# A four-layer window-attention kernel with its input, weights and output handed over in the layout of the chip's tiles

## The chip, the core and the metric

The kernel runs on one core of a Trainium2 chip. The metric is device time in microseconds (us), lower is better. The kernel before took 8497.35 us as the median of three runs (8497.1 to 8511.64).

Names used below: PE is TensorE (matmuls; PEld its weight loads), DVE is VectorE, ACT is ScalarE, POOL is GpSimd, SP is SyncE, which computes nothing and issues DMAs. ACT and POOL issue DMAs too. A row "SPq" or "ACTq" with DMA_DIRECT2D is the issue of transfers, not the transfer itself.

## What is computed

The input x is 16 images of 56 x 56 tokens with 96 channels, float32. Four transformer layers of shifted-window attention follow each other, each of this shape (layers differ in norm, number of heads and mask):

```
def layer(x, mask, qkv, table, proj, mlp):
    h = norm(x)                                      # layer 0: over the whole image; others: per token
    h = roll(h, (-3, -3)); xw = windows(h, 7, 7)     # 64 windows of 49 tokens per image
    q, k, v = split(xw @ qkv_w + qkv_b)              # 12, 12, 12 and 4 heads
    a = softmax(q @ k.T * scale + rel_bias(table) + mask)
    h = roll(unwindow((a @ v) @ proj_w + proj_b), (3, 3))
    x = x + h
    return x + (gelu(norm(x) @ w1 + b1) @ w2 + b2)   # layer 3 has one more norm before w2
```

The mask of layer 0 is an input (one 49 x 49 table for each window of each image); those of layers 1 to 3 are constants. The roll by (-3, -3) and the cut into windows are the same in all four layers.

## The kernel before

The 16 images are worked in four groups of four. The tile `x` holds two groups; in it a partition is one of 98 tokens (two windows side by side, 2 x 49) and the free dimension runs over the group's 128 window pairs and 96 channels. So the rolled and windowed form is made once, when x is loaded, and undone once, when the output is stored: everything between works in place. Four window pairs make a quad; an attention stage or an MLP stage of a layer is 32 quads. Each engine has its own program: `fill` for the first two quads, then a loop over the four groups with, for each layer, 32 quads of attention and 32 quads of MLP, software-pipelined (`quad_steps`, `rolled_steps`, `mlp_into_attention`). Within the loop PE, DVE, ACT and POOL hand tiles to each other by semaphores, and SP issues, for every attention quad, four copies `Vbd<-Vd` (L524) and in layer 0 two mask loads (`mask_quad`, L436).

Where x and the output move: `tokens` (L429) cuts four images by `runs` into 312 DMAs, each of 7, 4 or 3 partitions (a row of a window, or its two parts where the roll wraps) and up to 32 window pairs of 96 channels, 384 bytes a piece. The first group is loaded at the start, half of its DMAs by SP and half by ACT, images 0 and 1 first (`s_x0`), then images 2 and 3 (`s_x`). In the loop SP stores group g-1 after the spreads of layer 0's attention, and loads group g+1 after those of layer 1; both lie beside MLP stages, in which SP has no spreads to issue. At the very end SP stores images 0 and 1 of the last group while their last layer still runs for images 2 and 3, then waits for `s_fin` (the last group is finished) and stores images 2 and 3 together with ACT.

What precedes the loop: POOL sets the pads (memsets L560 to L568: the zeros around blocks of `mask0`, `Vbd` and the staged tables, and the ones that stand in as a bias row in `hT`, `OT`, `h4`), then issues the tables of relative bias (`load_bias`, L488: 49 DMAs a layer, 7 partitions each, straight from the 13 x 13 tables into their 49 x 49 form) and the weights of layer 2. SP and ACT issue the other weights (`load_weights`, L443, 18 DMAs a layer) and ACT the first table, behind their parts of x. Four copies `room<-room` (L579) double the staged tables to the second window's partitions (64 to 112). DVE takes the first mean and variance of each token as x lands (L1042, L1050, L1056; 32 quads), waits for all constants, folds the gain of layer 3's extra norm into `w3` (L1078 to L1088, with two short matmul groups L840 and L842 on PE between), and writes the bias tables (L1101: layer 0; L1103: layers 1 to 3, staged table plus constant mask, once for each of four mask cases and each of two windows, 49 partitions each; the source is read backwards along the keys). Then come the image norm of layer 0 (`norm`: L1137 to L1178 on DVE, averages L862 on PE behind warming matmuls L856, a power on POOL L588), the first ACT instruction (L745), and the loop.

Of the kernel before, what the change touches and what calls it, by code (L numbers as in the profile page):

```python
# [13 lines left out]
N = WS * WS  # L14
# [93 lines left out]

def build(nc, d, x_in, out):
    ctx = ExitStack()  # L110
    with ctx:
# [72 lines left out]
        s_braw0 = sem("first_bias_raw_loaded")  # L184
        s_bsec = sem("bias_raw_copied")
        s_tab = sem("bias_tables_ready")
        s_memset = sem("pads_set")
        s_x = sem("x_loaded")
        s_x0 = sem("first_images_loaded")
        s_const2 = sem("third_layer_loaded")  # L190
# [204 lines left out]
        def runs(first, last):  # L395

            A = NWR
            for r in range(WS):  # L400
                if r + SHIFT < WS:
                    rows = [(slice(first * A, last * A), first * H + r + SHIFT)]
                else:
                    rows = [(slice(m * A, m * A + A - 1), m * H + r + SHIFT) for m in range(first, last)]
                    rows.append((slice(first * A + A - 1, last * A, A), first * H + r + SHIFT - WS))
                for a, row in rows:
                    for w in range(2):
                        for j in range(4):
                            cut = WS if w == 0 else WS - SHIFT
                            q = N * w + WS * r  # L410
                            col = WS * (2 * j + w) + SHIFT
                            yield slice(q, q + cut), a, j, row, col
                            if w:
                                yield slice(q + cut, q + WS), a, j, row, (col + cut) % W

        def tokens(eng, g, store, s, first=0, last=IMGS, turn=0, turns=1):

            dram = out if store else x_in
            rows_of = x[:, bass.ds((g % 2) * NP, NP), :].rearrange("p (a j) c -> p a j c", j=4)
            for n, (q, a, j, row, col) in enumerate(runs(first, last)):  # L420
                if n % turns != turn:
                    continue
                step = a.step or 1
                count = len(range(a.start, a.stop, step))
                far = bass.AP(dram.tensor, g * (IMGS * H * W * C) + (row * W + col) * C,
# [11 lines left out]

        TOK_DMAS = len(list(runs(0, IMGS)))
        HALF_DMAS = len(list(runs(0, IMGS // 2)))
        n_const, n_const2 = [0], [0]  # L440

        def load(eng, dst, src):
            eng.dma_start(dst, src).then_inc(s_const, 16)  # L443
# [961 lines left out]
```

## Time and profile before

| | |
|---|---|
| median of three runs | 8497.35 us |
| profiled execution: its own time, and its span | 8497.1 us, 8497.1 us |
| PE busy | 7930.6 us, 93% of the span |
| DVE, POOL, ACT busy | 72%, 64%, 61% |
| DMA moved | 142.33 MB in 597322 packets, 596066 of them under 512 B |
| issues of x and the output | 312 DMAs for a group, each way |

The profiled execution has a span equal to its own time, so its rows can be laid against the time of the runs directly. The share of DMA in a row of windows is the mean busy share of the core's 16 DMA engines. Read the table with the stages in mind: the first 165.8 us and the last 44.6 us of the span have hardly any PE work in them, while the middle is a periodic loop.

### The profile page before, as it was taken

The numbers are of one execution on the slowest core, as the hardware profiler recorded it, in microseconds if no ns is written. First come the engines' busy times: TensorE is split into PE (matmuls) and PEld (weight loads), VectorE is DVE, ScalarE is ACT, GpSimd is POOL, SyncE is SP. The second block draws the span as 40 slices with busy tenths as digits, with TensorE's granted clock in tenths as the row PEclk, the third lists the DMA queues.
The fourth block names the chain that finished last, engine by engine and source line by source line (L and its number), as shares of the span: only waits on it lengthen the run. The fifth ranks groups of instructions, "written<-read, shape, count | busy, mean of one in ns | idle before, by whom it ended". The sixth has DMA issues, their size and how long they took to land.

```text
span 8497.1 us, 316211 instructions
## 1 busy us (share of the span) xinstructions
PE 7930.6 (93%) x111222; PEld 5968.4 (70%) x111222; DVE 6104.5 (72%) x18304; ACT 5155.3 (61%) x9130; POOL 5402.6 (64%) x6733
## 2 busy tenths in 40 slices
PE   2999999999999999999999999999999999999997
PEld 1777777777777777776767777777776777777766
DVE  3777767767777776776777677776677767777666
ACT  1755747646774664755767476574577647566456
POOL 6865646556785665655778465564678756566565
PEclk9999999999999999999999999999999999999998
DMA  3100010000011011000001101000101100000001
GB/s 42 22 13 10 15 27 15 10 12 13 10 21 31 13 20 23 15 7 16 9 15 21 28 15 28 15 15 4 20 3 21 26 21 15 6 14 13 7 17 23
DMA packets 597322, 142.33 MB, mean 17 GB/s; under 512 B 596066, under 2 KB 596662, under 8 KB 596877
## 3 DMA queue, kind: packets, MB, share of 16 engines
q1 hardware_dynamic: 574508, 131.49, 7.8%
q10 hardware_dynamic: 16865, 3.97, 0.3%
q8 instruction: 246, 4.03, 0.2%
q0 software_dynamic: 5504, 1.21, 0.1%
q14 instruction: 199, 1.63, 0.1%
HBM read 31.76 MB, written 19.27 MB: 6 GB/s over the span
## 4 chain that ended last, share of the span: by engine, by line
PE 70%; DVE 12%; issue 8%; ACT 3%; DVEq 3%; POOL 1%; POOLq 0%; ACTq 0%
PE ps L912 12%; PE ps L973 11%; PE ps L900 8%; PE ps L876 7%; PE ps L1016 7%; PE ps L989 7%; PE ps L919 5%; PE ps L942 3%; PE ps L952 3%; DVE bst L1042 3%; ACT PT L779 3%; PE ps L961 2%; DVE xn L1195 2%; PE ps L856 2%; DVE S L1244 2%
## 5 line engine op out<-in xcount | busy, mean ns | idle before, releaser
L643 POOL TENSOR_TENSOR S<-S,mx 113x588 f32<-113x588 f32 (+1 forms) x2048 | 2065.4, 1008 | 1528.3 <-DVE mx L1246 1524.5
L779 ACT ACTIVATE PT<-ps 98x588 f32<-98x588 f32 (+1 forms) x2048 | 1182.5, 577 | 1239.9 <-PE ps L973 1233.1
L912 PEld LDWEIGHTS ps<-Vbd,PT 98*49 98x49 f32 x40960 | 1113.0, 125 | 666.4 <-issue 642.7
L1244 DVE TENSOR_TENSOR S<-ps,bias 113x588 f32<-113x588 f32 (+1 forms) x1536 | 962.9, 627 | 856.7 <-PE ps L900 856.7
L912 PE MATMUL ps<-Vbd,PT 98*49 98x18 f32 (+1 forms) x40960 | 1326.7, 202 | 171.7 <-ACT PT L779 109.7
L1246 DVE TENSOR_REDUCE mx<-S 113x12 f32<-113x588 f32 (+1 forms) x2048 | 1359.6, 664 | 70.5
L973 PEld LDWEIGHTS ps<-ident,S 113*98 113x98 f32 x10240 | 1040.6, 128 | 473.1 <-issue 382.0
L973 PE MATMUL ps<-ident,S 113*98 113x113 f32 x10240 | 1346.0, 262 | 3.8 <-ACT S L761 3.4
L761 ACT ACTIVATE S<-S 113x588 f32<-113x588 f32 (+1 forms) x2048 | 1240.0, 605 | 54.4 <-POOL S L643 52.3
L989 PEld LDWEIGHTS ps<-w,G 128*98 128x98 f32 x12288 | 1151.1, 168 | 161.6 <-issue 89.5
L989 PE MATMUL ps<-w,G 128*98 128x96 f32 (+1 forms) x12288 | 1152.0, 250 | 0.8 <-DVE x L1329 0.8
L1016 PE MATMUL ps<-h,w 97*128 97x392 f32 x3072 | 1125.6, 503 | 9.1 <-ACT G L819 9.1
L900 PE MATMUL ps<-room,QT 32*64 32x196 f32 (+3 forms) x26624 | 1054.1, 311 | 11.1 <-issue 10.8
L1042 DVE BATCH_NORM_STATS2 bst<-x 98x6 f32 (+1 forms) x4224 | 869.7, 253 | 178.9 <-DMA x<-x_dram 80.4
L732 ACT ACTIVATE room<-ps,kmask 96x392 f32<-96x392 f32 x1540 | 887.5, 578 | 44.8 <-PE ps L876 44.8
L819 ACT ACTIVATE G<-ps 128x1176 f32<-128x1176 f32 x512 | 588.8, 1150 | 536.0 <-PE ps L1016 535.7
L876 PE MATMUL ps<-hT,wqkv 97*96 97x392 f32 (+1 forms) x2052 | 891.3, 517 | 18.7 <-ACT hT L784 10.1
L609 POOL TENSOR_TENSOR rstd<-rstd,neghalf 98x4 f32 (+1 forms) x768 | 787.6, 1025 | 143.9 <-POOL rstd L606 143.9
L1016 PEld LDWEIGHTS ps<-h,w 97*128 97x128 f32 x3072 | 549.4, 192 | 302.4 <-ACT G L819 12.3
L797 ACT ACTIVATE h<-ps,gb 96x392 f32<-96x392 f32 x512 | 345.5, 675 | 638.0 <-PE ps L1003 638.0
L627 POOL TENSOR_TENSOR G<-bias,mask 113x588 f32<-113x588 f32 x513 | 688.0, 1341 | 7.8 <-issue 7.6
L900 PEld LDWEIGHTS ps<-room,QT 32*64 32x64 f32 (+1 forms) x26624 | 443.6, 123 | 342.3 <-issue 340.6
(104 smaller groups left out, 10493.0 us busy)
## 6 DMA issues: line engine op xcount, KB each, us to landing
Vbd<-Vd SPq DMA_DIRECT2D x1536, 41.3 KB
Vbd<-Vd SPq DMA_DIRECT2D x512, 38.3 KB
mask<-L_conv_mask_matrix_dram SPq DMA_DIRECT2D x258, 37.5 KB
x<-x_dram SPq DMA_DIRECT2D x48, 84.0 KB
out_dram<-x SPq DMA_DIRECT2D x48, 84.0 KB
x<-x_dram SPq DMA_DIRECT2D x228, 10.5 KB
out_dram<-x SPq DMA_DIRECT2D x228, 10.5 KB
out_dram<-x SPq DMA_DIRECT2D x180, 18.4 KB
```

Source lines behind the costliest of these rows:

```text
L643: pool.tensor_tensor(v, v, m, ALU.subtract).then_inc(a_sub, 1)
L761: act.activation(S[:, e, 0:nh * N], S[:, e, 0:nh * N], ACT.Exp).then_inc(a_exp, 1)
L779: act.activation(PT[:, (s + 3) % 4, 0:blocks, :, :].rearrange("p (b t) w n -> p b (t w) n", b=banks), PTps[:, PT_BANK[l] - 3:PT_BANK[l] - ...
L876: return pe.matmul(dst[0:at.stop - at.start, :], wqkv[:, at], hT[:, :, :, :].rearrange("p j w n -> p (j w n)"), start=True, stop=True)
L900: last = pe.matmul(out, q, keys, start=True, stop=True)
L912: last = pe.matmul(Ops[ROW2 * w:ROW2 * w + N, p, b, :].rearrange("p (a n) -> p a n", a=2), PT[:, p, b, w, :], v, start=True, stop=True)
L973: last = pe.transpose(at.rearrange("p w q -> p (w q)")[:, 0:TOK], S[:, e, PAIR * b:PAIR * (b + 1)], ident[0:TOK, 0:TOK])
L989: last = pe.matmul(ps[0:PAIR, 6 + t, wide * j:wide * j + weights.shape[1]], G[:, t, c, PAIR * j:PAIR * (j + 1)], weights, start=(c == 0), ...
L1016: last = pe.matmul(ps[:, 2 + c, 0:QUAD * PAIR], w1[:, l, P * c:P * (c + 1)], h4[:, s, :, :].rearrange("p a q -> p (a q)"), start=True, sto ...
L1042: last = dve.bn_stats(bst[:, t, j, :], x[:, half + (at + j), :])
L1244: dve.tensor_tensor(dst, scores, b, ALU.add).then_inc(a_bi, 1)
L1246: dve.reduce_max(mx[:, e, 0:nh], S[:, e, 0:n].rearrange("p (h k) -> p h k", k=N), axis=AX.X).then_inc(a_mx, 1)
```

## The change

The host hands over x already rolled, cut into windows and laid out as [group, 98 partitions, 128 pairs x 96], and takes the output back in that layout (`to_windows`, `from_windows`). So `tokens` is one DMA for each image: 98 partitions of 32 x 96 floats (12,288 contiguous bytes), four for a group instead of 312. The weights of all layers are handed over side by side, with each bias vector as row 97 of its matrix: `wqkv` is one DMA of 97 partitions x 1216 floats, `w1` one of 97 x 1536, `wp` one of 97 x 384; `w2`, `c2`, `gb`, `gb3` are one DMA each. Layer 0's bias table comes finished (`bias0`, 128 x 588), the others as one staged tile (128 x 1372), with both windows' rows in it and the keys in order, so the copies `room<-room` and layer 0's table copy are gone and DVE adds the constant masks over all 128 partitions at once. The mask of layer 0 is laid out so that a partition's four windows are contiguous. POOL keeps three small memsets; the pads of `mask0`, `hT`, `OT`, `h4` and `Vbd` are set by DVE at the head of its program. Neither the host's packing nor its unpacking is in the device time.

```
     def tokens(eng, g, store, s, first=0, last=IMGS, turn=0, turns=1):
         dram = out if store else x_in
-        rows_of = x[:, bass.ds((g % 2) * NP, NP), :].rearrange("p (a j) c -> p a j c", j=4)
-        for n, (q, a, j, row, col) in enumerate(runs(first, last)):
-            if n % turns != turn:
...
-            far = bass.AP(dram.tensor, g * (IMGS * H * W * C) + (row * W + col) * C,
-                          [[C, q.stop - q.start], [step * WS * W * C, count], [1, C]])
-            near = rows_of[q, a, j, :]
+        for image in range(first, last):
+            if image % turns != turn:
+                continue
+            at = slice(image * PAIRS_IMG, (image + 1) * PAIRS_IMG)
+            far = dram[g, :, at.start * C:at.stop * C]
+            near = x[:, (g % 2) * NP + at.start:(g % 2) * NP + at.stop, :].rearrange("p a c -> p (a c)")
             dst, src = (far, near) if store else (near, far)
             eng.dma_start(dst, src).then_inc(s, 16)
...
     def _(sp):
         tokens(sp, 0, False, s_x0, 0, IMGS // 2, turn=0, turns=2)
         tokens(sp, 0, False, s_x, IMGS // 2, IMGS, turn=0, turns=2)
-        load(sp, ident[:, :], d["ident"])
-        load(sp, kmask[:, :], d["kmask"])
         load(sp, average[:, :], d["average"])
-        sp.wait_ge(s_memset, 1)
-        for l in (0, 3):
-            load_weights(sp, l, load)
...
+        load(sp, w1[:, :, :].rearrange("p l n -> p (l n)"), d["w1"])
+        load(sp, c2[:, :, :].rearrange("p l n -> p (l n)"), d["c2"].to_broadcast([P, LAYERS * C]))
+        load(sp, gb3[:, :, :].rearrange("p j c -> p (j c)"), d["gb3"])
+        sp.wait_ge(s_maskpad, 1)
...
     def _(pool):
-        for t in (mask0, room, Vbd):
-            pool.memset(t[:], 0.0)
...
-        for l in range(1, LAYERS):
-            load_bias(pool, l, s_braw)
...
-        for l in range(LAYERS):
-            pool.dma_start(stage(l)[ROW2:ROW2 + N, :], stage(l)[0:N, :]).then_inc(s_bsec, 16)
+        pool.wait_ge(s_memset, 2)
...
     def _(act):
-        act.wait_ge(s_memset, 1)
-        load_bias(act, 0, s_braw0)
-        load_weights(act, 1, load)
+        load(act, ident[:, :], d["ident"])
+        load(act, kmask[:, :], d["kmask"])
+        load(act, wqkv[:, :], d["wqkv"])
+        load(act, gb[:, :, :].rearrange("p l j -> p (l j)"), d["gb"])
+        load(act, wp[:, :, :].rearrange("p l n -> p (l n)"), d["wp"])
+        load(act, w2[:, :, :, :].rearrange("p l c n -> p (l c n)"), d["w2"])
+        load(act, bias[0][:, 0, :], d["bias0"])
+        load(act, mask4[:, :, :].rearrange("p a b -> p (a b)"), d["mask4"])
+        act.dma_start(room[:, 0:STAGED], d["bias"]).then_inc(s_braw, 16)
...
     def _(dve):
+        dve.memset(mask0[:], 0.0).then_inc(s_maskpad, 1)
+        for t in (hT, OT, h4):
+            dve.memset(t[:], 1.0)
+        dve.memset(Vbd[:], 0.0).then_inc(s_memset, 1)
         dve.wait_ge(s_x0, 16 * HALF_DMAS)
...
-        for l in range(LAYERS):
+        for l in range(1, LAYERS):
             nh = HEADS[l]
-            for v in range(1 if l == 0 else 4):
-                for w in range(2):
-                    r = slice(ROW2 * w, ROW2 * w + N)
-                    dst = bias[l][r, v, :].rearrange("p (h k) -> p h k", k=N)
-                    src = stage(l)[r, :].rearrange("p (h k) -> p h k", k=N)[:, :, ::-1]
...
+            for v in range(4):
+                last = dve.tensor_tensor(bias[l][:, v, :].rearrange("p (h k) -> p h k", k=N),
+                                         stage(l).rearrange("p (h k) -> p h k", k=N),
+                                         mask4[:, v, :].unsqueeze(1).to_broadcast([P, nh, N]), ALU.add)
```

How the order of instructions moves is shown at three places. In the rows, "7x2x96 x2" is the shape of one DMA (partitions first) and how many follow each other.

The end of ACT's issues before the loop, in the kernel before (the last of its 156 DMAs for x, the table of layer 0, the weights of layer 1, and its first computing instruction):

```order
L429 DMA x<-x_dram 7x2x96 x2
L429 DMA x<-x_dram 3x2x96 x4
L488 DMA room<-L_conv_rel_bias_table_dram 7x12x7 x49
L443 DMA wqkv<-L_conv_qkv_w_dram 96x96 x2
L443 DMA wqkv<-L_conv_qkv_w_dram 96x6x8 x2
L443 DMA wqkv<-L_conv_qkv_b_dram 1x96 x2
L443 DMA wqkv<-L_conv_qkv_b_dram 1x6x8 x2
L443 DMA wp<-L_conv_proj_w_dram 96x96
L443 DMA wp<-L_conv_proj_b_dram 1x96
L443 DMA w<-L_conv_mlp_w_dram 96x384
```

The whole of ACT's issues before the loop in the changed kernel:

```order
L460 DMA x<-x_dram 98x3072 x2
L473 DMA ident<-k_ident_dram 128x128
L473 DMA kmask<-k_kmask_dram 96x4
L473 DMA wqkv<-wqkv_dram 97x1216
L473 DMA gb<-gb_dram 96x16
L473 DMA wp<-wp_dram 97x384
L473 DMA w<-w_dram 128x1152
L473 DMA bias<-bias_dram 128x588
L473 DMA G<-k_mask_dram 128x196
L693 DMA room<-bias_dram 128x1372
L721 ACT_TABLE_LOAD
L721 ACTIVATE xn<-x,nmr,vpe 98x384
```

ACT issues 11 DMAs in place of 223 there; the weights of all layers stand in tiles of 96, 97 or 128 partitions.

DVE between the token statistics and the loop, before (`gb`, `w`: layer 3's extra norm; `bias<-room,G`: the tables, `G` holding the constant mask):

```order
L1078 MEMSET room 128x128
L1079 MEMSET w 128x3
L1081 COPY room<-gb 128x128 x3
L1083 TENSOR_SCALAR w<-w,gb 128x96 x3
L1086 TENSOR_TENSOR w<-w,ps 128x3x96
L1088 TENSOR_TENSOR c<-c,ps 128x96
L1101 COPY bias<-room 49x588 x2
L1103 TENSOR_TENSOR bias<-room,G 49x588 x16
L1103 TENSOR_TENSOR bias<-room,G 49x196 x8
L1204 MEMSET Vd 98x48
```

The same place in the changed kernel, from the last two steps of the norm's part:

```order
L1063 TENSOR_TENSOR w<-w,ps 128x3x96
L1065 TENSOR_TENSOR c<-c,ps 128x96
L1071 TENSOR_TENSOR bias<-room,G 128x588 x8
L1071 TENSOR_TENSOR bias<-room,G 128x196 x4
L1173 MEMSET Vd 98x48
```

Twelve additions over 128 partitions stand for twenty-four additions and two copies over 49.

The end of SP's program before, after the last spread (the last rows of its stores of images 2 and 3):

```order
L429 DMA out_dram<-x 7x7x96 x2
L429 DMA out_dram<-x 4x7x96 x4
L429 DMA out_dram<-x 7x2x96 x2
L429 DMA out_dram<-x 4x2x96 x4
L111 UNCONDITIONAL_BRANCH
```

The end of SP's program in the changed kernel:

```order
L511 DMA Vbd<-Vd 49x4x50 x4
L306 REGISTER_ALU
L306 COMPARE_AND_BRANCH
L511 DMA Vbd<-Vd 49x4x50 x4
L460 DMA out_dram<-x 98x3072 x3
L168 UNCONDITIONAL_BRANCH
```

Three DMAs (images 0, 1 and 2; image 3 is ACT's one) stand where SP had 234. Inside the loop PE, DVE, ACT and POOL have the same instructions in the same order as before; on SP only `tokens` and the shape of the mask loads differ.

## Rows read from the trace of the kernel before

**Rows 1.** The page: span, busy time, PE and DMA in 40 slices.

```profile
span 8497.1 us, 316211 instructions
PE 7930.6 (93%) x111222; PEld 5968.4 (70%) x111222; DVE 6104.5 (72%) x18304; ACT 5155.3 (61%) x9130; POOL 5402.6 (64%) x6733
PE   2999999999999999999999999999999999999997
DMA  3100010000011011000001101000101100000001
```

**Rows 2.** Waits, whole run: engine line waited for: us in total, times, longest.

```profile
ACT L745 <- DVE nmr L1178: 165.8, 1, 165.8
DVE bst L1042 <- DMA x<-x_dram: 80.4, 2, 56.1
```

**Rows 3.** Timeline, start of the program: start us, us, what, [idle before <- releaser].

```profile
0.76 90.71 SPq L429 DMA_DIRECT2D x<-x_dram  x156
...
56.09 1.38 DVE L1042 BATCH_NORM_STATS2 bst<-x 98x6 f32<-98x96 f32 x8 [56.09 <-DMA x<-x_dram]
...
79.44 0.17 DVE L1056 COPY mv<-agg 98x8 f32<-98x8 f32 x1
...
103.93 1.38 DVE L1042 BATCH_NORM_STATS2 bst<-x 98x6 f32<-98x96 f32 x8 [24.32 <-DMA x<-x_dram]
...
127.24 0.17 DVE L1056 COPY mv<-agg 98x8 f32<-98x8 f32 x1
...
135.02 0.17 DVE L1078 MEMSET room<- 128x128 f32 x1 [7.62 <-DMA gb<-L_conv_norm_b_dram]
...
139.71 0.93 DVE L1101 COPY bias<-room 49x588 f32<-49x588 f32 x2
...
156.23 0.10 DVE L1204 MEMSET Vd<- 98x48 f32 x1
```

**Rows 4.** Groups by form, 0 to 170 us: x count | busy us, mean ns.

```profile
L1103 DVE TENSOR_TENSOR bias<-room,G 49x588 f32<-49x588 f32 x16 | 12.3, 766 | 0.2
L1103 DVE TENSOR_TENSOR bias<-room,G 49x196 f32<-49x196 f32 x8 | 2.9, 357 | 0.1
L1164 DVE TENSOR_SCALAR ivar<-ps 98x4 f32<-98x4 f32 x1 | 0.2, 161 | 3.4 <-PE ps L862 3.4
```

**Rows 5.** The line of DVE's largest memset: duration ns min/median/max.

```profile
L1208 DVE MEMSET ps<- x16: 485/485/485, 174.6 to 7990.1; 128x512 f32 x16
```

**Rows 6.** Windows: PE, PEld, DVE, ACT, POOL busy, PE clock, DMA share, GB/s.

```profile
12.00:22.00 10.00, 0.00 (x0) 0.00 (x0) 0.00 (x0) 0.00 (x0) 9.69 (x21) 1.00 0.44 62
104.00:105.00 1.00, 0.00 (x0) 0.00 (x0) 1.00 (x7) 0.00 (x0) 1.00 (x3) 1.00 0.86 146
131.00:132.00 1.00, 0.00 (x0) 0.00 (x0) 0.00 (x0) 0.00 (x0) 0.00 (x0) 1.00 0.86 289
140.00:160.00 20.00, 8.59 (x14) 3.67 (x15) 17.44 (x33) 0.00 (x0) 0.00 (x0) 0.76 0.00 0
8455.00:8495.00 40.00, 0.00 (x0) 0.00 (x0) 0.00 (x0) 0.00 (x0) 0.00 (x0) 0.50 0.26 58
```

**Rows 7.** DMA issues, 0 to 170 us: count, KB each, median us to landing.

```profile
room<-conv_rel_bias_table_dram POOLq DMA_DIRECT2D x98, 2.3 KB, 3.2
room<-room POOLq DMA_DIRECT2D x3, 112.5 KB, 2.7
```

**Rows 8.** Timeline, end of the program.

```profile
8449.37 1.36 DVE L1329 SCALAR_TENSOR_TENSOR x<-ps,r,x 98x96 f32 x4
...
8452.51 42.68 SPq L429 DMA_DIRECT2D out_dram<-x  x78
```

**Rows 9.** Windows: the MLP stage of layer 0 in groups 0 and 3, of layer 1 in groups 0 and 3.

```profile
567.00:719.00 152.00, 141.06 (x1050) 111.04 (x1049) 103.70 (x437) 58.84 (x65) 68.90 (x96) 1.00 0.00 0
...
6779.00:6931.00 152.00, 141.37 (x1051) 111.34 (x1052) 104.78 (x439) 58.65 (x65) 70.36 (x96) 1.00 0.13 27
1103.00:1250.00 147.00, 141.23 (x1047) 111.04 (x1048) 101.73 (x430) 58.60 (x65) 72.18 (x99) 1.00 0.16 27
7315.00:7462.00 147.00, 141.25 (x1048) 111.08 (x1049) 101.57 (x430) 58.63 (x65) 72.58 (x99) 1.00 0.00 0
```

**Rows 10.** SP's timeline around the load of group 1.

```profile
1001.73 83.64 SPq L524 DMA_DIRECT2D Vbd<-Vd  x32
1085.41 112.21 SPq L429 DMA_DIRECT2D x<-x_dram  x228
```

More of the change, by code:

```diff
@@ new lines, in packed @@
+def packed(inputs):
+    out = {"x": to_windows(inputs["x"])}
+    m = inputs["L0_conv_mask_matrix"].reshape(B * PAIRS_IMG, 2, N, N).transpose(1, 2, 0, 3)
+    out["mask"] = m.reshape(2, N, B * PAIRS_IMG * N)
+    qkv, p, m1, m2, last, gains, bias = [], [], [], [], [], [], []
+    for l in range(LAYERS):
+        w = {r: inputs[n] for r, n in names(l).items()}
+        if l == 2:
+            w = {r: a.T if r in ("wqkv", "wp", "w1", "w2") else a for r, a in w.items()}
+        full = np.concatenate([w["wqkv"], w["bqkv"][None]])
+        dh = C // HEADS[l]
+        for j in range(2):
+            part = full[:, C * j:C * (j + 1)]
+            if HEADS[l] == 4:
+                part = np.pad(part.reshape(C + 1, 4, dh), ((0, 0), (0, 0), (0, GRP - dh))).reshape(C + 1, P)
+            qkv.append(part)
+        v = full[:, 2 * C:].reshape(C + 1, HEADS[l] // 2, 2, dh)
+        qkv.append(v.transpose(0, 2, 1, 3).reshape(C + 1, C))
+        p.append(np.concatenate([w["wp"], w["bp"][None]]))
+        m1.append(np.concatenate([w["w1"], w["c1"][None]]))
+        m2.append(w["w2"].reshape(HC, P, C).transpose(1, 0, 2).reshape(P, HC * C))
+        last.append(w["c2"])
+        gains += [w["g1"], w["b1"], w["g2"], w["b2"]]
+        t = w["table"][index_of_bias()].transpose(0, 2, 1).reshape(N, HEADS[l] * N)
+        rows = np.zeros((P, HEADS[l] * N), np.float32)
+        rows[0:N], rows[ROW2:ROW2 + N] = t, t
+        bias.append(rows)
+    out["wqkv"] = np.concatenate(qkv, axis=1)
+    out["wp"], out["w1"], out["w2"] = (np.concatenate(a, axis=1) for a in (p, m1, m2))
+    out["c2"] = np.concatenate(last)[None]
+    out["gb"] = np.stack(gains, axis=1)
+    out["gb3"] = np.concatenate([inputs[n].reshape(HC, P).T for n in ("L3_conv_ln3_g", "L3_conv_ln3_b")], axis=1)
+    out["bias0"] = bias[0]
+    out["bias"] = np.concatenate(bias[1:], axis=1)
+    return out
@@ L444, in load @@
             n_const[0] += 16
[L446 to L488 removed]
+        STAGED = sum(HEADS[1:]) * N
+        def stage(l):
+            return room[:, sum(HEADS[1:l]) * N:sum(HEADS[1:l + 1]) * N]
         @block.sync
@@ L1400 @@
         d[name] = d.pop("k_" + name)
[L1401 removed]
+    out = nc.dram_tensor("out_0_dram", (GROUPS, PAIR, NP * C), F32, kind="ExternalOutput").ap()
     build(nc, d, d["x"], out)
     r = _run(nc, [arrays], core_ids=[0])
[L1404 removed]
+    return from_windows(np.asarray(r.results[0]["out_0_dram"]))
```

126 lines of the change are left out of this document (23 added, 103 removed).

## The prediction, made before the changed kernel ran

> **What bounds the kernel now.** I read the page first [rows 1]. PE is busy 93% of the span and no other engine passes 72%, so in the middle of the program only PE's work counts. But the 40 slices of PE read 2, then 9 throughout, then 7: the first slice of 212 us is mostly empty, and so is part of the last. The change touches only DMAs and what surrounds them, so those two ends are where to look.
>
> The list of waits names the front end [rows 2]: ACT's first instruction waits 165.8 us, and DVE waits 80.4 us in two pieces for x. The timeline of the start shows how these come about [rows 3]. SP issues its 156 DMAs for x in 90.71 us (0.58 us each), as ACT does beside it. DVE can begin the token statistics of images 0 and 1 at 56.09, ends them at 79.61, and waits for images 2 and 3 until 103.93; those statistics end at 127.41. The last constant (layer 1's `gb`, issued by ACT behind its x and the table of layer 0) lets DVE go on at 135.02. Then come 4.69 us of folding the extra norm of layer 3 (to 139.71), 16.5 us of bias tables (to 156.23), and 9.55 us of image norm, to 165.78.
>
> The timeline of the end [rows 8]: DVE's last residual of layer 3 ends at 8450.73, SP and ACT begin to issue images 2 and 3 at 8452.51, and the span ends at 8497.1, so 44.6 us of pure output stand behind the last arithmetic. The profiled execution's own time is its span, 8497.1, and the median is 8497.35, so the sum below needs no correction.
>
> **The middle of the program: nothing.** In the loop SP issues x and the output after its last spread of a stage: the load of group 1 follows 32 spread DMAs directly, takes 112.21 us [rows 10], and lies beside an MLP stage of 147 us, so SP is free again before the next spread is due. Did the transfers themselves slow the stage? Layer 1's MLP in group 0 runs with such a load beside it (DMA share 0.16) and in group 3 with none (0.00): 1047 matmuls and 141.23 us of PE against 1048 and 141.25 [rows 9]. Layer 0's MLP without a store in group 0 and with one in group 3: 141.06 against 141.37. So the 312 issues cost the loop nothing now, and removing them gives nothing. The mask loads keep their number. Instructions on the other engines are unchanged. What can get worse is the intensity, a rival below.
>
> **The transfer of x at the start.** An image is 98 partitions x 12,288 bytes = 1.204 MB; four are 4.82 MB. How many DMA engines carry a DMA from SP or ACT? While both issue only pieces of 7, 4 and 3 partitions the share is 0.44, that is 7 of 16 engines (0.4375), and while tiles of 96 and 128 partitions are in flight it is 0.86 [rows 6]. I read this as: a DMA is dealt to its engines in equal whole numbers of partitions. 98 partitions then go to 14 engines, 7 each: 86 KB an image on each engine, 172 KB for two images, 344 KB for four.
>
> At what rate? At the end of the program, with 384-byte pieces, 58 GB/s at a share of 0.26 is 13.9 GB/s for a busy engine (27.6 ns a piece). With the 2,352-byte rows of `room<-room` it is 289 GB/s at 0.86, or 21.0 GB/s (112 ns) [rows 6]. A fixed part and a part by size through these two points give 0.043 ns a byte, so my estimate for rows of 4.9 to 12 KB is 23 GB/s an engine. As fixed time of a DMA I take 3.2 us from issue to landing, from the small table DMAs [rows 7]. So images 0 and 1 are in at 0.8 + 172/23 + 3.2 = 11.5 us instead of 56.09. The two statistics stretches (23.52 and 23.48 us, [rows 3]) then follow each other without a gap and end at 58.5.
>
> **DVE's pads** stand ahead of this: 392 + 392 + 392 + 784 + 1728 elements a partition at 485 ns for 512 [rows 5] are 3.5 us, over before x lands at 11.5. If that cover were gone they would cost 3.5. POOL's memsets never held anybody and give nothing back.
>
> **The weights are the next late thing.** `wqkv`, `w1` and `wp` now have 97 partitions, and 97 has no divisor that is 16 or less but 1. Dealt as above, all of 97 x 4,864 + 97 x 6,144 + 97 x 1,536 = 1.217 MB goes through one engine, which also carries its 344 KB of x and about 81 KB of the 128-partition constants due before `s_const`: 1,642 KB. SP's `w1` and ACT's `wqkv` and `wp` are on two queues but, so read, on the same engine, so they add. At 23 GB/s: 0.8 + 71.4 + 3.2 = 75.4 us, behind the statistics at 58.5. The start is thus bound by one DMA engine. The staged tables (44 KB more on it, 1.9 us) land within the 4.69 us of folding. Bounds: if the 97 partitions spread over the engines, the constants are in well before 58.5; if the engine keeps the 13.9 GB/s of small pieces, they are in at 122.1.
>
> The Trainium skill, "DMA: Bandwidth & Descriptors" (section "Why a DMA increments its semaphore by 16 and not by 1"), states such a rule: the number of engines is the largest up to 16 that divides the slowest dimension of both sides, with 127 partitions as an example for one engine. The share of 0.44 agrees for 7 partitions; no row shows 97. By the rule the sum is the one I take, without it that of the second case below. The same page puts an engine at about 27 GiB/s (29 GB/s); an estimate by that would be constants at 60.6 us and 8378 us in all.
>
> **From the constants to the loop.** Folding stays 4.69 us. Tables: before, 16 additions at 766 ns, 8 at 357 and two copies [rows 4]. Now 8 and 4 over 128 partitions; free size and operation are the same, so 8 x 0.766 + 4 x 0.357 = 7.6 us instead of 16.5. At the price of the copies (0.93 us for two, [rows 3]), were the backward read what made them slow, they would be some 3 us cheaper; if the cost rose with partitions (128/49), 12 us dearer. I take equal, since free size sets all of DVE's durations that I see. The norm stays 9.55. In it DVE waits 3.4 us for PE's warming matmuls and average [rows 4], in a stretch where the granted clock is 0.76 on average [rows 6], a mixture of full and half (2.4 and 1.2 GHz), after PE had stood idle for the tables. With shorter tables PE idles less; 0 to 2 us may come back, I count 0.
>
> So the loop starts at 75.4 + 4.7 + 7.6 + 9.5 = 97.2 instead of 165.8: 68.6 us less.
>
> **The end.** Images 0 and 1 are stored under the last MLP stage, as before. For images 2 and 3, 172 KB an engine: 7.5 + 3.2 = 10.7 us after 8452.51 instead of 44.6: 33.9 less. At 13.9 GB/s it is 15.6, so 29.0 less. Sum: 8497.1 - 68.6 - 33.9 = 8394.6 us.
>
> **Rivals.**
> 1. *One engine carries the 97-partition weights* (the forecast): 8395. For it: the shares. Against: it rests on pieces of 7 partitions.
> 2. *The weights spread; DVE's statistics bind.* Constants are in before 58.5, and the loop starts at 58.5 + 21.8 = 80.3: 85.5 + 33.9 less, 8378. For it: 0.86 with large tiles, partly from POOL's queue, whose dealing may differ.
> 3. *Long rows bring no better rate.* 13.9 GB/s: constants at 122.1, loop at 143.9, 21.9 + 29.0 less, 8446. Against: the 21.0 GB/s of the copies; for it: those are between tiles of the chip, not from memory.
> 4. *Slower: the single engine takes its rows one after another, with their latency.* ACT's queue holds 194 such rows (`wqkv`, `wp`). At the 2.7 us from issue to landing of the large copies [rows 7] a row, constants come at about 528 us and the time is about 8847. It decides from 0.9 us a row in ACT's queue, where the start is 34 us later than now and eats the gain at the end. Against: 62 GB/s over 7 engines in 384-byte pieces is one in 43 ns an engine [rows 6], far below any latency.
> 5. *The bursts in the loop stop PE.* A group now moves in about 4.82 MB / (14 x 23 GB/s) = 15 us, at twice the share seen beside PE or more. Six and a half such bursts with PE standing throughout cost 97 us: 8492, no change. Against: rows 9, which see no loss at all at the lower intensity.
>
> **How the numbers follow.** The forecast has 68 in 100, the second case 17, the third 8, the fourth 2, the fifth 2; 3 are left for mixtures. Predicted is the forecast's 8394. Its own unknown is the engine's rate: at 17 GB/s it gives constants at 100.6, a tail of 13.3 and 8422. Downward the second case with 4 us less for tables and norm gives 8374. The range 8373 to 8422 leaves out cases 3 to 5. 0.2% is 17 us, about what a measurement of this kernel can tell from no change: faster by more holds for cases 1 to 3 and the mixtures, 96 in 100; within it case 5, 2; slower case 4, 2.
>
> **What would show it.** Right: ACT's first instruction near 97 us; DVE's first statistics near 11 with a single wait for x, a gap of some 17 us between the last statistics (58) and L1055, put down to a DMA; 7.6 us of L1071; in the windows from 25 to 75 us a DMA share near 1/16 with 20 to 25 GB/s; a last store issued about 11 us before the end; a group's period unchanged. If the share stays high until the constants are in, near 30 us, and L1055 follows the statistics at once, the second case holds. If the window after 25 us shows 14 GB/s or less, the third. The prediction is wrong in kind if the MLP stages of layers 0 and 1 grow, or if the loop starts after 165.8.

## The result, and the profile after

| | before | after |
|---|---|---|
| median (lowest to highest) of 4 runs each | 8501.19 us (8497.1 to 8511.64) | 8372.33 us (8370.18 to 8374.06) |
| span of the profiled execution | 8497.1 us | 8371.6 us |
| start: ACT's first instruction | 165.8 us | 91.8 us |
| from there to the issue of the last stores | 8286.7 us | 8269.8 us |
| from there to the end | 44.6 us | 10.0 us |

After over before is 0.9847, with a 95% interval of 0.9833 to 0.9861: the changed kernel is faster by 1.5%. The spans differ by 125.5 us, and the table divides them: 74.0 at the start, 16.9 in the loop, 34.6 at the end. The prediction had 68.6, nothing and 33.9, in all 8394 with a range of 8373 to 8422. (The medians of the four runs differ by 128.9.) So the time is 22 us better than predicted and just under the range. Most of the miss is the 16.9 us of the loop, where the prediction saw nothing to gain: without them the time would be 8389, 5 us better than predicted and inside the range.

The page of the changed kernel (answers to [rows 1]):

```profile
span 8371.6 us, 313958 instructions
PE 7933.7 (95%) x111222; PEld 5970.4 (71%) x111222; DVE 6097.4 (73%) x18295; ACT 5156.9 (62%) x9130; POOL 5299.7 (63%) x6553
PE   6999999999999999999999999999999999999998
```

PE has the same 111,222 matmuls and 3 us more busy time than before, in a span 125 us shorter; the first slice of PE went from 2 to 6. All of the gain is idle time of PE.

Its waits, whole run (answers to [rows 2]; engine, line, what it waited for, us in total, times, longest):

```profile
ACT L721 <- DVE nmr L1147: 91.8, 1, 91.8
DVE room L1055 <- DMA G<-k_mask_dram: 13.2, 1, 13.2
DVE bst L1017 <- DMA x<-x_dram: 7.9, 1, 7.9
```

The two waits for x (80.4 us) became one of 7.9, and a wait for the constants, 13.2 us, is there in its place.

Its timeline of the start (answers to [rows 3]; start us, us, what, idle before and its releaser). x12 in the row at 77.43 counts both forms:

```profile
0.76 0.84 SPq L460 DMA_DIRECT2D x<-x_dram  x2
...
2.37 26.94 SPq L473 DMA_DIRECT2D c<-c_dram  x1
3.25 29.74 ACTq L473 DMA_DIRECT2D gb<-gb_dram  x1
3.26 1.50 DVE L1049 MEMSET Vbd<- 98x1728 f32 x1 [0.31 <-issue]
12.61 1.38 DVE L1017 BATCH_NORM_STATS2 bst<-x 98x6 f32<-98x96 f32 x8 [7.86 <-DMA x<-x_dram]
...
36.05 1.38 DVE L1017 BATCH_NORM_STATS2 bst<-x 98x6 f32<-98x96 f32 x8
36.44 25.40 ACTq L473 DMA_DIRECT2D w<-w_dram  x1
...
59.32 0.17 DVE L1031 COPY mv<-agg 98x8 f32<-98x8 f32 x1
...
62.52 0.48 ACTq L473 DMA_DIRECT2D G<-k_mask_dram  x1
63.03 0.48 ACTq L693 DMA_DIRECT2D room<-bias_dram  x1
72.75 0.17 DVE L1055 MEMSET room<- 128x128 f32 x1 [13.25 <-DMA G<-k_mask_dram]
...
77.43 6.63 DVE L1071 TENSOR_TENSOR bias<-room,G 128x588 f32<-128x588 f32 x12
...
88.68 0.16 DVE L1133 TENSOR_SCALAR ivar<-ps 98x4 f32<-98x4 f32 x1 [1.37 <-PE ps L837]
```

The second half of the statistics follows the first at 36.05 without a gap. They end at 59.5, and DVE then stands until 72.75. Three issues last 25 to 30 us each, and one of ACT (`wp`) and five of SP behind the first of them 3.4 us each, where the others last 0.2 to 0.6. The trace names nothing that an issue waits for; that it waits for room in a queue is a reading. So the last constants, `G` and the staged tables, were issued only at 62.52 and 63.03, and landed some 10 and 11 us later.

Windows of the changed kernel (columns as in [rows 6]), of the start, the norm and the end:

```profile
5.00:10.00 5.00, 0.00 (x0) 0.00 (x0) 0.00 (x0) 0.00 (x0) 0.00 (x0) 1.00 0.86 297
15.00:20.00 5.00, 0.00 (x0) 0.00 (x0) 3.96 (x32) 0.00 (x0) 0.00 (x0) 1.00 0.77 243
50.00:55.00 5.00, 0.00 (x0) 0.00 (x0) 3.71 (x28) 0.00 (x0) 0.00 (x0) 1.00 0.06 26
...
80.00:92.00 12.00, 11.61 (x27) 4.94 (x26) 7.42 (x20) 0.24 (x1) 2.90 (x3) 1.00 0.00 1
8365.00:8371.00 6.00, 0.00 (x0) 0.00 (x0) 0.00 (x0) 0.00 (x0) 0.00 (x0) 0.50 0.68 262
```

Two plateaus: up to 20 us most engines work, and at 50 us the share is 0.06, one engine of 16, moving 26 GB/s. By the Trainium skill's "DMA: Bandwidth & Descriptors" (section "Why a DMA increments its semaphore by 16 and not by 1") 97 partitions go to a single engine, since 97 has no divisor up to 16 but 1; the 0.06 agrees. At the end (0.68, 262 GB/s) the stores of images 2 and 3 take 10.0 us in place of 44.6 [rows 8].

The loop is where the unexpected part lies. Windows from the first to the last matmul of `h` times `w1` in the MLP stages of layers 0, 2 and 1, first group; the kernel before (for layers 0 and 1 this is [rows 9] cut exactly):

```profile
567.09:719.17 152.08, 141.15 (x1050) 110.98 (x1049) 103.61 (x437) 58.75 (x65) 68.98 (x96) 1.00 0.00 0
1635.84:1785.22 149.38, 140.51 (x1046) 110.56 (x1044) 101.28 (x430) 58.52 (x64) 71.85 (x99) 1.00 0.00 0
1103.27:1250.07 146.80, 141.03 (x1046) 110.77 (x1044) 101.46 (x429) 58.55 (x64) 72.22 (x99) 1.00 0.15 27
```

and the changed kernel:

```profile
489.31:637.45 148.14, 141.15 (x1050) 110.99 (x1049) 103.95 (x438) 58.52 (x64) 70.58 (x96) 1.00 0.00 0
1553.00:1700.85 147.85, 140.71 (x1045) 110.61 (x1044) 101.42 (x430) 58.53 (x64) 72.34 (x99) 1.00 0.00 0
1022.08:1168.42 146.34, 140.53 (x1046) 110.58 (x1045) 101.22 (x429) 58.52 (x64) 72.09 (x99) 1.00 0.00 0
```

The same matmuls, the same PE busy time, no DMA beside them in layers 0 and 2, full clock; yet layer 0's stage is 3.9 us shorter and layer 2's 1.5, while layer 1's hardly differs. Over the four groups the stages of layer 0 add up to 14.0 us and those of layer 2 to 6.0 us less; the rest of the loop gives back 3 to 4. Where in a stage? One turn of the two-quad loop of layer 0, DVE's normalization at the turn, in the kernel before:

```profile
628.25 1.40 DVE L1195 TENSOR_SCALAR xn<-x,mv,vpe 98x96 f32 x4 [0.72 <-issue]
...
629.70 0.54 PE L1003 MATMUL ps<-ident,xn 98*96 98x98 f32 x4 [0.56 <-DVE xn L1195]
```

and after:

```profile
548.71 1.39 DVE L1164 TENSOR_SCALAR xn<-x,mv,vpe 98x96 f32 x4 [0.55 <-issue]
...
550.16 0.54 PE L978 MATMUL ps<-ident,xn 98*96 98x98 f32 x4 [0.30 <-DVE xn L1164]
```

"issue" means that DVE waited for nothing that the profile shows: it is the time in which it branches back to the head of its loop and the next instruction begins. It is 0.17 us shorter, PE's wait for `xn` is 0.26 us shorter, and a turn of PE (two quads) takes 9.34 us instead of 9.58. The loop makes 13 such turns in a stage; each is at least 0.24 us shorter, the first two 0.38 and 0.54, and together they are the 3.9 us. Nothing in the code of the loop accounts for it: DVE's instructions and their order are the same.

The records of DVE's sequencer in the same traces show two places where the time goes. From the end of the branch back to the beginning of the next instruction pass 0.26 us before and 0.11 after. And one of the four statistics of the turn's second quad begins 0.10 us later before than after, so that the four take 1.01 us instead of 0.91:

```profile
625.66 1.01 DVE L1042 BATCH_NORM_STATS2 bst<-x 98x6 f32 x4
```

```profile
546.40 0.91 DVE L1017 BATCH_NORM_STATS2 bst<-x 98x6 f32 x4 [0.16 <-DVE x L1319]
```

The two together are the 0.24 us of a turn.

### The profile page after: what moved, and what is told of

The parts are those of the page before. It is cut to its first block, busy times and chain, and to the rows that moved or that the text cites. A ratio compares the mean times of both kernels' runs of the same rounds, so it can differ in the third digit from the quotient of the medians.

```text
span 8371.6 us, 313958 instructions
## 1 busy us (share of the span) xinstructions
PE 7933.7 (95%) x111222; PEld 5970.4 (71%) x111222; DVE 6097.4 (73%) x18295; ACT 5156.9 (62%) x9130; POOL 5299.7 (63%) x6553
## 4 chain that ended last, share of the span: by engine, by line
PE 68%; DVE 12%; issue 9%; POOL 4%; ACT 3%; DVEq 3%; POOLq 0%; ACTq 0%
PE ps L887 12%; PE ps L948 10%; PE ps L991 7%; PE ps L964 7%; PE ps L875 7%; PE ps L851 7%; PE ps L894 5%; PE ps L917 3%; PE ps L927 3%; DVE bst L1017 3%; ACT PT L755 2%; POOL G L597 2%; PE ps L936 2%; DVE xn L1164 2%; PE ps L831 2%
## 5 line engine op out<-in xcount | busy, mean ns | idle before, releaser
L875 PE MATMUL ps<-room,QT 32*64 32x196 f32 (+3 forms) x26624 | 1054.1, 311 | 11.5 <-issue 11.2
## 6 DMA issues: line engine op xcount, KB each, us to landing
room<-bias_dram ACTq DMA_DIRECT2D x1, 686.0 KB, 11.3
```

Of the source, the lines that this page charges most:

```text
L875: last = pe.matmul(out, q, keys, start=True, stop=True)
```

## Experiments

The theories on the loop, before any experiment: **P**, what changed is where DVE's loops stand in its stream of instructions (DVE executes 567 instructions ahead of its first clearing of PSUM before, 556 after, and the loops are moved by as many); **T**, the lighter DMA traffic or SP's shorter program does it. On the start: **S**, one engine carries the 97-partition weights and everything behind them; against it, that x's transfer or DVE's own work sets the start.

"Loop" below is the time from the start of the first score matmul to the start of the last matmul of `h` times `w1`: 8259.3 us before, 8242.6 after, in the profiled executions. Eight of the runs only add instructions that do nothing (`stand`: an increment of a semaphore that nobody waits for) to DVE's program ahead of everything.

**e1: after, with DVE's loops put back to the place that they had before.**

```diff
     def _(dve):
+        for _ in range(11):
+            stand(dve)
         dve.memset(mask0[:], 0.0).then_inc(s_maskpad, 1)
```

> The changed kernel with 11 idle semaphore increments at the head of DVE's program, where DVE waits for x anyway, so that DVE's loops stand at the same place in its instruction stream as in the kernel before (by the two traces DVE executes 567 instructions ahead of its first L1208 before, 556 after). Theory P (the loop got 17 us shorter because DVE's code moved and its jump back fetches differently): layer 0's MLP stages grow from 148.1 to about 152 us, layer 2's from 147.9 to 149.4, and the time rises by 10 to 20 us to about 8388. Theory T (the loop got shorter because of fewer and larger transfers): stages stay at 148.1 and 147.9, time 8372. Start and end stay as in the changed kernel (91.8 and 10 us).

Measured: median 8385.23 us (8384.5 to 8388.16), 0.9863 of before (0.9846 to 0.9879); loop 8258.1. ACT starts at 90.8, so the eleven instructions cost the start nothing. The stages of layers 0 and 2 are back at the length of before:

```profile
490.01:642.02 152.01, 141.14 (x1050) 110.97 (x1048) 104.52 (x438) 58.54 (x64) 69.85 (x96) 1.00 0.00 0
1558.67:1708.08 149.41, 140.51 (x1046) 110.57 (x1045) 101.34 (x430) 58.54 (x64) 71.81 (x99) 1.00 0.00 0
```

Eleven idle instructions in 8,370 us take back 15.5 of the 16.7 us. Theory T is refuted: the traffic here is that of after, the loop that of before. The 1.2 us left are within what kernels with the same place differ by (see below).

**e2: before, with DVE's loops moved on by 245.** If only the place modulo some power of two counts, 245 = 256 - 11 puts them where they are after.

```diff
     def _(dve):
+        for _ in range(245):
+            stand(dve)
         dve.wait_ge(s_x0, 16 * HALF_DMAS)
```

> The kernel before with 245 idle semaphore increments at the head of DVE's program, ahead of its first wait for x (56 us long, so they should be hidden); 245 is 256 less 11, so if a place in the instruction stream counts modulo 256 instructions or a divisor of it, DVE's loops stand as in the changed kernel. Theory P: layer 0's MLP stages fall from 152 to about 148 us, layer 2's from 149.4 to 147.9, the time to about 8480. Theory T: no change, 8497 to 8505. If neither and the place matters in another way, the stages move by another amount.

Measured: 8479.41 us (8477.23 to 8487.34), 0.9976 of before (0.9966 to 0.9986); loop 8240.9. The two stages, in the kernel with the old DMAs:

```profile
564.62:712.81 148.19, 141.15 (x1049) 110.99 (x1048) 103.99 (x438) 58.45 (x64) 70.48 (x96) 1.00 0.00 0
1628.27:1776.51 148.24, 141.16 (x1045) 110.75 (x1044) 101.51 (x430) 58.49 (x64) 72.23 (x99) 1.00 0.00 0
```

The kernel before gains the whole of the loop's difference without any part of the change (layer 2's stage is 148.2 us in the first group, 147.4 to 147.9 in the other three). P holds in both directions.

**p8 to p256: after, with 8, 16, 32, 64, 128 and 256 idle instructions** (as e1, with another number; each ran once).

> The same with 8 increments (564). If blocks are of 8 or fewer instructions, the stages are those of the changed kernel (148.1, 147.9); if they are of 16 or more, they differ by 1 to 4 us in layer 0 or 2, as 11 increments did. The transfers are the same in all, so any difference is one of place.

> The changed kernel with 16 idle semaphore increments at the head of DVE's program (572 DVE instructions ahead of the first L1208's counterpart in place of 556). If DVE's fetch after the jump back of a loop goes in blocks of 16 instructions or fewer, the loops stand in their blocks as in the changed kernel and layer 0's MLP stage stays at 148.1 us, layer 2's at 147.9, time 8372; if blocks are larger, the stages move, to anything between 148 and 152.

> The changed kernel with 32 idle semaphore increments at the head of DVE's program (588 DVE instructions ahead of the first clear of PSUM in place of 556). 8 and 16 increments both lengthened layer 0's MLP stage to about 151.5 us, 256 less 11 on the kernel before did not. If the place counts modulo 32, layer 0's MLP stays at 148.1 and layer 2's at 147.9; if not, 151 to 152 and 149.4.

> The same with 64 increments (620). Modulo 64 or 32: 148.1 and 147.9. If this one and the one with 32 are both long, the period is 128 or 256 instructions.

> The changed kernel with 128 idle semaphore increments at the head of DVE's program (684 in place of 556). Modulo 128: the MLP stages are the changed kernel's, 148.1 us in layer 0, 146.4 in layer 1, 147.9 in layer 2. Modulo 256: at least one of them differs by over 1 us.

> The same with 256 increments (812). By either reading the stages are the changed kernel's: 148.1, 146.4, 147.9; the time is about 8372 if the increments end before x lands at 12.6 us, and later by what they take beyond that. If the stages differ, the place doesn't count modulo 256 and the match of the kernel before with 245 was chance.

Measured (stages of the first group, from windows as above):

| idle instructions | time | loop | MLP of layer 0, 1, 2 |
|---|---|---|---|
| 0 (after) | 8372.33 | 8242.6 | 148.1, 146.3, 147.9 |
| 8 | 8380.56 | 8249.8 | 152.3, 146.4, 149.4 |
| 11 (e1) | 8385.23 | 8258.1 | 152.0, 146.8, 149.4 |
| 16 | 8385.96 | 8255.0 | 152.0, 146.4, 149.8 |
| 32 | 8387.24 | 8256.3 | 151.5, 146.4, 146.8 |
| 64 | 8384.93 | 8254.1 | 151.7, 148.1, 146.4 |
| 128 | 8375.45 | 8244.4 | 148.2, 146.5, 147.7 |
| 256 | 8373.65 | 8238.8 | 148.1, 146.4, 147.8 |

The lengths of all three stages come back at 128 and at 256 and at no smaller number, and each stage has its own good and bad places. One number is not exact: the stages of layer 0 differ by up to 1.6 us from group to group in the same run (148.1, 149.2, 149.8, 148.1 in after), and over all four groups they add up to 594.4 to 595.2 us with 0, 128 and 256, and to 601.6 to 609.0 with the five others. 64 is the telling one: layer 0 is bad, layer 1 becomes bad, layer 2 is better than ever. The whole-run sum of DVE's idle time ahead of this instruction follows: the rows of before, of after, and of 64. With 128 it is 140.0 us again.

```profile
DVE xn L1195 <- issue: 150.8, 324, 0.7
```

```profile
DVE xn L1164 <- issue: 139.9, 320, 0.7
```

```profile
DVE xn L1166 <- issue: 157.9, 326, 1.2
```

So the place counts modulo 128 instructions of DVE. The sequencer's records say more than the lengths. The loop of an MLP stage is 64 DVE instructions long. In the first group of every run, counting the instructions of a turn from 0, one of them begins late or none does, and the branch back takes more or less time with it (the number after the semicolon: from the end of the branch to the next beginning):

| DVE instructions ahead | runs | layer 0 | layer 1 | layer 2 |
|---|---|---|---|---|
| 556, 684, 812 | after, e3, e5, b2, b3; 128; 256, e2 | none; 0.11 | none; 0.13 | no. 17; 0.22 to 0.24 |
| 544 | b1 | none; 0.13 | none; 0.13 | none seen; 0.24 |
| 564 | 8 | no. 57; 0.26 | none; 0.13 | no. 9; 0.24 |
| 567 | before, e1, e4 | no. 54; 0.26 | none; 0.13 | no. 6; 0.24 |
| 572 | 16 | no. 49; 0.26 | none; 0.13 | no. 1; 0.24 |
| 588 | 32 | no. 33; 0.26 | none; 0.13 | none; 0.13 |
| 620 | 64 | no. 1; 0.26 | no. 41; 0.24 | none; 0.13 |

The late instruction begins about 0.10 us late (0.03 in layer 0 with 8). In each layer its number and the number of instructions ahead add up to the same sum, modulo 128: 621, 661 and 573. By that sum b1's layer 2 should have its pause at no. 29, where none is seen, though its branch back is long. So the pause stands at a fixed place of DVE's stream, one every 128 instructions; a 64-instruction loop either holds such a place or does not, and one that does also branches back 0.10 to 0.15 us later. Layer 2's loop holds one both before and after; there it moved from no. 6, within the four `xn` that PE waits for, to no. 17, a statistic, and the stage is 1.5 us shorter. What in the chip stands behind these places no run shows, nor whether the other engines have them.

Kernels with the same place agree: the eight with loops at 556, 684 or 812 have 8238.7 to 8244.4 us from first to last, the three at 567 have 8258.1 to 8260.6. The 256 also show that idle instructions are not free: they end at 26.2 us, the pads behind them when x has long landed, and the statistics end behind the constants; the start is 4 us later.

**e3: after, the three 97-partition loads cut into 96 and 1.** Its DVE program is unchanged, so its loops stand where those of after stand.

```diff
-        load(sp, w1[:, :, :].rearrange("p l n -> p (l n)"), d["w1"])
+        for rows in (slice(0, C), slice(C, C + 1)):
+            load(sp, w1[rows, :, :].rearrange("p l n -> p (l n)"), d["w1"][rows, :])
```

(and likewise `wqkv` and `wp` on ACT)

> The changed kernel with wqkv, w1 and wp each loaded as two DMAs, 96 partitions and 1 partition, in place of one of 97. Theory E (97 partitions go through one DMA engine and that sets the start): the DMA share no longer sits near 1/16 from 20 to 60 us, the constants are in before DVE's statistics end at 58.5, L1055 follows at about 59.5 without a wait, ACT's first instruction at about 78.5 in place of 91.8, time 8359. Theory B (the start is bound by the bytes or the issue of these loads, not by the engine): L1055 stays near 72 and the time near 8372.

Measured: 8360.21 us (8357.97 to 8362.99), 0.9834 of before (0.9818 to 0.9851), 12 us better than after; ACT starts at 80.6, loop 8238.7. Its windows and its issues:

```profile
5.00:10.00 5.00, 0.00 (x0) 0.00 (x0) 0.00 (x0) 0.00 (x0) 0.00 (x0) 1.00 1.02 263
30.00:35.00 5.00, 0.00 (x0) 0.00 (x0) 3.86 (x32) 0.00 (x0) 0.00 (x0) 1.00 0.80 274
```

```profile
2.90 0.36 SPq L473 DMA_DIRECT2D c<-c_dram  x1
...
3.58 0.32 ACTq L473 DMA_DIRECT2D gb<-gb_dram  x1
...
61.59 0.17 DVE L1058 MEMSET room<- 128x128 f32 x1
```

The share stays high until everything is in (0.80 from 30 to 35 us, 0.03 from 35 to 40). The same issues of `c` and `gb` take 0.36 and 0.32 us in place of 26.94 and 29.74, and L1058 (L1055 of after) follows the statistics with no wait. S holds: the single engine bound the start of the changed kernel. How much of it was its own transfers and how much the issues held up behind them, this run doesn't separate. What it gave is not the 13.2 us of the wait but 11.2: the statistics begin at 14.66 instead of 12.61, with x and the weights now on the same engines.

**e4: before, with only x and the output in the new layout** (`tokens`, `to_windows`, `from_windows` of after; weights, tables, pads as before).

> The kernel before with only x and the output in the layout of windows (four DMAs a group); weights, tables, pads and masks as before. Statistics end at about 60 us; POOL's 147 table DMAs at 0.56 us and its weights then set the constants at about 108, the loop starts at about 139 (27 us earlier than before), the tail falls to 10 us. Theory P: the loop is as long as before, time about 8436. Theory T (the transfers of x shortened the loop): 17 us less, 8419.

Measured: 8440.6 us (8435.11 to 8442.89), 0.9926 (0.991 to 0.9943); start 142.0, loop 8260.6, that of before, as P has it for a DVE program whose loops stand at 567. DVE waits 12.6 us for x, and then:

```profile
DVE room L1066 <- DMA gb<-L_conv_norm_b_dram: 50.6, 1, 50.6
```

x alone brings 23.8 us of the 74.0 at the start; then the constants are late, at 110.17: POOL issues its 147 table DMAs until 98.33 and its weights until 108.35. The end, 10.2 us from the issue of the last stores, is that of after.

**e5: the counterpart, after with x and the output in the old layout.**

> The changed kernel with x and the output as before (312 DMAs a group), weights, tables, masks and pads as changed. The x DMAs fill SP and ACT to about 91 us; only then are the weights issued, with the 97-partition ones on one engine for 1.2 MB / 26 GB/s = 47 us, the rest behind them: constants at about 150 us, the loop starts at about 169 in place of 165.8, the tail is 44.6. Theory P (place in DVE's stream, as in the changed kernel): loop 17 us shorter than before, time about 8484. Theory T (transfers of x shorten the loop): loop as before, about 8500.

Measured: 8464.72 us (8460.95 to 8470.62) where 8484 was expected, 0.9959 (0.9945 to 0.9973); start 149.1 where some 169 was expected, loop 8240.1. The loop is short with the 312 DMAs in it: P again. The two halves of the change don't add up: x alone brings 23.8 us at the start, everything else alone 16.7, both 74.0, since with either alone the other is what comes last. The start was mis-estimated. SP's issues of x:

```profile
0.77 72.54 SPq L484 DMA_DIRECT2D x<-x_dram  x156
```

The same 312 DMAs take 72.5 us here and 90.71 before [rows 3]. Before, POOL's table DMAs, also of 7 partitions, ran beside them; here there are none. That these were on the same seven engines fits the shares (0.37 here between 12 and 22 us, 0.44 before) but was not separated from other differences of the two kernels.

**b1: a better version, first try.** e3, the tables on POOL, the folding moved between the halves of the statistics, and the last store cut: image 2 goes as soon as it is finished, image 3 in halves on SP and ACT.

```diff
+            pool.wait_ge(s_braw, 16)
+            pool.wait_ge(s_const, ALL_CONST)
+            for l in range(1, LAYERS):
+                for v in range(4):
+                    last = pool.tensor_tensor(bias[l][:, v, :]..., stage(l)..., mask4[:, v, :]..., ALU.add)
...
+            sp.wait_ge(m_res, GROUPS * LAYER_QUADS - NQ // 4)
+            tokens(sp, GROUPS - 1, True, s_out, IMGS // 2, IMGS - 1)
             ...
-            tokens(sp, GROUPS - 1, True, s_out, IMGS // 2, IMGS, turn=0, turns=2)
+            last_half(sp, 0)
```

> A version built on the loads in 96 and 1 partitions: POOL, idle at the start, makes the bias tables while DVE takes the statistics (12 additions, hidden; saves DVE 6.7 us); the first half of folding layer 3's norm comes between the two halves of the statistics, so that PE's 3 us of answer are hidden; at the end image 2 is stored by itself when it is done and image 3 in two halves by SP and ACT (tail 10 to about 6.5 us). Against 8360 of the loads in 96 and 1: 8360 - 6.7 - 3 - 3.5 = 8347, if DVE's loops stand well; if their place (12 instructions and some waits fewer) falls badly, up to 17 more, 8364. If POOL and DVE disturb each other in the statistics, DVE's statistics grow above 23.5 us a half.

Measured: 8364.49 us (8363.4 to 8368.21), 0.9841 (0.9825 to 0.9858), where 8347 was expected: no better than e3, though the end alone gives 3.8 us. The end is 6.2 us in place of 10.0. The start is 82.5, later than e3's 80.6, though DVE has 6.6 us less to do:

```profile
35.39 12.39 POOL L568 TENSOR_TENSOR bias<-room,G 128x588 f32<-128x588 f32 x12 [34.47 <-DMA room<-bias_dram]
40.58 2.64 DVE L1081 COPY room<-gb 128x128 f32<-128x128 f32 x2
43.14 3.15 DVE L1083 TENSOR_SCALAR w<-w,gb 128x96 f32<-128x96 f32 x3
```

While POOL adds, DVE's copies take 2.64 us for two (0.35 in after) and its three products 3.15 us (0.62 in after). Later DVE waits 5.4 us for the first average, which PE gives behind its warming matmuls. The loop is 8245.7: this DVE program is 12 instructions shorter (544 ahead), and layer 0's first stage (149.3) is again another; its branch back takes 0.13 us, with no late instruction.

**b2: b1 with the folding back in its place and 12 idle instructions for the 12 additions.**

> b3 with the bias tables made by POOL during DVE's second half of statistics, the fold left where it was (in the combined version it collided with POOL and took 7 us in place of 1), the first group of PE's warming matmuls ahead of the first average left out (there DVE waited 5.4 us for it), and 12 idle increments on DVE for the 12 additions taken away, so that its loops stand at 556. Start 80.6 - 6.6 = 74 to 76, time 8350. If the loop is longer than 8242, place was not restored; if the start is near 80, something else (PE, POOL) took the tables' place.

Measured: 8355.66 us (8348.31 to 8358.36), 0.9823 (0.9807 to 0.984); start 80.3, loop 8242.8. The place is right again, but the statistics end at 65.8 instead of 61.5 in e3: they begin 0.9 us later, and take 3.4 us longer with POOL's additions beside them. In the norm DVE waits 3.4 us for PE where it had waited 1.4. So nearly all of the 6.6 us taken from DVE are given back.

**b3: only e3's cut and the cut last store.**

> The loads in 96 and 1 partitions (8360), and only the end changed: image 2 is stored by itself when its last quad is done, image 3 in two halves by SP and ACT. The tail falls from 10.0 to 6.2 us as in the combined version; DVE's program is untouched, so the loop stays at about 8239 us: 8356.

Measured: 8354.61 us (8353.31 to 8356.84), 0.9825 of before (0.9808 to 0.9841); start 80.2, loop 8241.4, end 6.2:

```profile
8348.82 0.32 SPq L467 DMA_DIRECT2D out_dram<-x  x1
```

in a span of 8355.0. It is 18 us below the changed kernel, 8356 was expected. b2 cannot be told from it, and b3 is the simpler one.

## Why the prediction was right and wrong

**The middle of the program: nothing. This step failed.** It put at zero what measured 16.9 us, the larger part of the miss of 22 us. What it said about the DMAs stands: e5 has all 312 of them and the short loop, e1 none of them and the long one. What it overlooked is that "the same instructions in the same order" is not the same place. Pads, statistics, folding and tables at the head of DVE's program set where its loops begin, modulo 128 instructions. In layer 0 that sets how long the branch back takes (0.26 us before, 0.11 after) and takes a pause of 0.10 us out of the loop; in layer 2 it moves the pause to where PE does not wait for it. The trace of before holds both pauses, but one kernel alone doesn't tell that they stay put while the code moves. What could have been had is the size of the unknown, the 150.8 us of "issue" ahead of one DVE line, and with it a wider range on both sides.

**The transfer of x.** Expected at 11.5 us, seen at 12.6, on 14 engines (0.86 between 5 and 10 us), with one wait and no gap between the halves. The pads ended at 4.8, hidden.

**The weights are the next late thing.** The mechanism was right, and e3 shows it by removing it. Constants were expected at 75.4, and came at 72.75; the gap was 13.2 us and not 17. Two errors met here, and that the number is so near is in part luck. The engine makes 26 GB/s and not 23, by which the prediction's own sum would give 67.2. And one part of the mechanism was not foreseen: ACT and SP stood 25 to 30 us at an issue, so `G` was issued only at 62.52, behind the bulk on the one engine and not beside it, and landed 5.6 us after the 67.2. The 686 KB of tables landed 11.3 us after their issue, and were still hidden under the folding: L1071 follows it without a wait.

**From the constants to the loop.** Tables 7.6 expected, 6.7 measured: each large addition lasts what it lasted before (764 ns on 128 partitions, 766 on 49 [rows 4]), but one begins 0.68 us after the other, where it was 0.78. So neither the partitions nor the backward read made an instruction longer; which part of the change brought them closer together is open. The norm was counted at 9.55 with 0 to 2 us possibly coming back; it took 7.6. DVE waits 1.4 us for the average instead of 3.4 [rows 4], and the granted clock is 1.00 in this stretch, not 0.76 [rows 6]: ahead of its first average PE now stood idle 0.39 us, before 11.41. This too was the possibility named and not taken. Constants 2.7, tables 0.9 and norm 1.9 make the start 5.4 us better than said.

**The end.** 10.0 us, expected 10.7.

**The rivals.** The weights on one engine won; the spread case (8378) is nearly e3 with the failed step taken out: 8360.2 + 16.7 = 8377, with its loop starting at 80.6 where the case had 80.3. Rows did not fall to latency, the engine did not stay at 13.9 GB/s, and bursts did not stop PE. The load of a group is now over in some 20 us, between 1004 and 1024 us, ahead of layer 1's MLP stage. Windows of the changed kernel, 22 us there and the same place of group 3, which loads nothing:

```profile
1000.00:1022.00 22.00, 21.30 (x332) 16.05 (x333) 16.34 (x43) 10.25 (x18) 9.74 (x13) 1.00 0.71 227
7202.48:7224.48 22.00, 21.30 (x332) 16.05 (x333) 16.34 (x43) 10.26 (x18) 9.75 (x13) 1.00 0.05 10
```

PE is as busy with 0.71 of the DMA engines at work as with hardly any.

## What to carry to other kernels

A bias row appended to a matrix makes 97 partitions of 96, and such a tile goes through one DMA engine at 26 GB/s and stops the issuing engines as well: cut it into 96 and 1. Few large DMAs for what is exposed at both ends of a program are worth what the two ends show in the timeline, and what lies beside a bound engine is worth nothing. When a change alters the number of instructions ahead of a hot loop on the engine that the bound engine waits for, that alone can move the time, here by up to 0.2%; tell it apart with a run that only pads. To see it in a trace, compare the same turn in both kernels for an instruction that begins late and for the time behind the branch back. No run here chose the place for the best time.

## What the runs showed of the hardware

- DVE's loop turn depends on where the loop stands modulo 128 of its instructions: stages with the same work take 148.1 or 152.0 us (layer 0), 146.4 or 148.1 (layer 1), 146.4 to 149.8 (layer 2), first group.
- In DVE's stream of instructions there is one place in every 128 at which one begins some 0.10 us late, and an MLP loop of 64 that holds it takes 0.22 to 0.26 us behind its branch back instead of 0.11 to 0.13 (layers 0 to 2 of the first group, all 16 traces; the late instruction is not seen in one of them, b1's layer 2).
- The issue of a 6 KB DMA took 29.74 us behind DMAs that lie on one engine, 0.32 us when these were spread.
- One DMA engine moves 26 GB/s with rows of 1.5 to 6 KB (share 0.06), and 14 move 297 GB/s (share 0.86), 21 GB/s each, while x's rows of 12 KB come in.
- Additions on POOL slow DVE beside them: three products of 128x96 took 3.15 us instead of 0.62, two copies 2.64 instead of 0.35.
- An addition of 588 elements a partition takes DVE as long on 128 partitions as on 49: 764 and 766 ns.
